# Cross attention: exponentials head by head with a bias, in place of a subtraction on GpSimd

## The reference, cut to what matters

```python
scores = jnp.einsum('bhqd,bhkd->bhqk', Q, K) / np.sqrt(D_K)      # layer 0, D_K = 16
scores = jnp.where(m == 0, NEG, scores)                          # NEG = -1e9
scores = jnp.einsum('bhtd,bhsd->bhts', qh, kh) * scale + mask    # layer 1
attn = jax.nn.softmax(scores, axis=-1)                           # over the 77 context tokens
x = jnp.einsum('bhqk,bhkd->bhqd', attn, V)
```

## Time and profile before

| | us |
|---|---|
| median of 3 runs | 1243.11 (1241.47 to 1243.6) |
| the profiled execution, its own time | 1242.15 |
| span of the trace, first to last instruction | 1240.4 |
| PE busy | 1064.9 (86%) |
| DVE busy | 959.5 (77%) |
| ACT busy | 693.5 (56%) |
| POOL busy | 383.5 (31%) |

### The profile page before, as it was taken

The page is one execution under the profiler, slowest core; times in us unless marked ns, Lnnn a source line. Parts: engine busy times, 40 slices in busy tenths (PEclk is TensorE's granted clock), DMA queues, the critical chain, the costliest instruction groups (busy, mean ns, idle before and its releaser), DMA issues. The chain is left out here.

```text
span 1240.4 us, 30089 instructions
## 1 busy us (share of the span) xinstructions
PE 1064.9 (86%) x10763; PEld 855.5 (69%) x10763; DVE 959.5 (77%) x2126; ACT 693.5 (56%) x1461; POOL 383.5 (31%) x535
## 2 busy tenths in 40 slices
PE   5899989989998799986279999489999859998696
PEld 3578878778787577765267777377788637776585
DVE  7588878877887588997838884569998648898597
ACT  3354544444545255555637776368778626555584
POOL 5123222221230256552220000423421225655232
PEclk9899999999999899997569999699999969999899
DMA  7000000200000230004336531300000000000011
GB/s 263 10 10 2 10 13 2 84 3 2 3 2 2 87 121 12 22 9 174 136 110 246 178 110 49 112 18 19 29 14 21 1 14 24 12 22 10 18 56 47
DMA packets 33493, 64.29 MB, mean 52 GB/s; under 512 B 7524, under 2 KB 23268, under 8 KB 30308
## 3 DMA queue, kind: packets, MB, share of 16 engines
q1 hardware_dynamic: 31844, 58.57, 13.5%
q0 software_dynamic: 1536, 4.20, 1.0%
HBM read 43.03 MB, written 12.39 MB: 45 GB/s over the span
## 5 line engine op out<-in xcount | busy, mean ns | idle before, releaser
L1151 ACT ACTIVATE ca_pth<-ca_turned 77x512 f16<-77x512 f32 x128 | 75.9, 593 | 99.8 <-PE ca_turned L1293 99.8
L395 ACT ACTIVATE wa_probs<-wa_scores,wa_minus_top 128x192 f32<-128x192 f32 x256 | 83.3, 437 | 80.5 <-DVE wa_minus_top L488 80.5
L1094 POOL TENSOR_TENSOR ca_z<-ca_z,ca_top 128x308 f32<-128x308 f32 x128 | 88.2, 701 | 112.4 <-DVE ca_top L1189 112.4
L351 POOL TENSOR_TENSOR wa_q<-wa_by_cos,wa_by_sin 128x256 f32<-128x256 f32 x32 | 23.4, 732 | 265.4 <-DVE wa_by_sin L483 265.4
L1194 DVE SCALAR_TENSOR_TENSOR ca_ptl<-ca_turned,ca_pth 77x512 f16<-77x512 f32 x128 | 87.0, 680 | 20.0 <-ACT ca_pth L1151 20.0
L1293 PE MATMUL ca_turned<-ident,ca_probs 128*77 128x128 f32 x512 | 87.0, 294 | 14.0 <-ACT ca_probs L1143 13.9
L406 ACT ACTIVATE wa_pth<-wa_turned 128x384 f16<-128x384 f32 x128 | 58.4, 506 | 72.2 <-PE wa_turned L715 72.2
L1293 PEld LDWEIGHTS ca_turned<-ident,ca_probs 128*77 128x77 f32 x512 | 57.7, 152 | 44.6 <-ACT ca_probs L1143 24.6
L640 PE MATMUL wa_scores<-wa_xh,wa_wh 128*128 128x256 f16 x256 | 71.1, 278 | 10.4 <-DVE wa_wl L467 8.8
L488 DVE TENSOR_REDUCE wa_minus_top<-wa_scores 128x2 f32<-128x384 f32 x128 | 62.3, 548 | 20.6 <-PE wa_scores L703 18.5
L715 PE MATMUL wa_turned<-ident,wa_probs 128*128 128x128 f32 x512 | 68.3, 275 | 7.8 <-ACT wa_probs L395 3.9
(11 more groups left out here) (388 smaller groups left out, 3643.8 us busy)
## 6 DMA issues: line engine op xcount, KB each, us to landing
ex_stage<-in_ew SPq DMA_DIRECT2D x16, 1024.0 KB, 7.0
slots<-slots_zeros SPq DMA_DIRECT2D x10, 512.0 KB, 6.2
ca_xs<-tokens SPq DMA_DIRECT2D x16, 256.0 KB, 2.4
ex_xe<-slots SPq DMA_DIRECT2D x11, 320.0 KB, 3.3
slots<-ex_y SPq DMA_DIRECT2D x9, 320.0 KB
wa_x_stage<-in_xt SPq DMA_DIRECT2D x8, 256.0 KB, 3.1
tokens<-in_x SPq DMA_DIRECT2D x1, 2048.0 KB, 15.3
ca_w<-in_xw SPq DMA_DIRECT2D x2, 1024.0 KB, 6.9
```

What stands on the lines that cost most here:

```text
L395: ins = act.activation(probs[2 * (u % 2) + t][:, h, t * WINDOW:t * WINDOW + SPAN], s_bank[i][:, t * SPAN:(t + 1) * SPAN], ACT.Exp, bias=mi ...
L1094: pool.tensor_tensor(z[k][:, heads], z[k][:, heads], top[:, k, heads].unsqueeze(2).broadcast_to((P, UH, CTX)), ALU.subtract).then_inc(shif ...
L1151: act.activation(pth[k][0:CTX], t_bank[k][0:CTX], ACT.Copy, scale=PSCALE).then_inc(probs_high, 1)
```

## The change

- POOL's `subtract` is gone, and with it the semaphore `shift`.
- DVE's maximum is written with its sign turned (`negate=True`) into a tile that is now called `minus_top`.
- The exponentials of a unit are four instructions, one for each head (77 values), each with the head's column of `minus_top` as its bias. They wait for the maximum itself (`maxed`). Only the last of the four tells PE (`exped`).
- In layer 0 the factor 1/4 moves from the exponential to the masking, which becomes a `scalar_tensor_tensor` like that of layer 1; the constant for masked scores is then -1e9 in place of -4e9.

```diff
@@ gpsimd
-            def subtract(b, c):
-                pool.wait_ge(maxed, b * PAIRS + c // 2 + 1)
-                k = c // 2 % 2
-                heads = slice(UH * (c % 2), UH * (c % 2 + 1))
-                pool.tensor_tensor(z[k][:, heads], z[k][:, heads], top[:, k, heads].unsqueeze(2).broadcast_to((P, UH, CTX)),
-                                   ALU.subtract).then_inc(shift, 1)
...
-                    if c < UNITS - 2:
-                        subtract(b, c + 2)
-                    elif after:
-                        subtract(b + 1, c + 2 - UNITS)
@@ scalar, power
-                act.wait_ge(shift, b * UNITS + c + 1)
+                act.wait_ge(maxed, b * PAIRS + c // 2 + 1)
                 if not (first(b) and c < 2):
                     act.wait_ge(probs_t, b * UNITS + c - 1)
-                act.activation(probs[k][:], z[c // 2 % 2][:, UH * k:UH * (k + 1)], ACT.Exp, scale=1.0 if additive else CD ** -0.5).then_inc(exped, 1)
+                for h in range(UH):
+                    n = UH * k + h
+                    ins = act.activation(probs[k][:, h], z[c // 2 % 2][:, n], ACT.Exp, bias=minus_top[:, c // 2 % 2, n:n + 1])
+                ins.then_inc(exped, 1)
@@ vector, mask_scores and take_maximum
-                if additive:
-                    ins = dve.scalar_tensor_tensor(out=z[k][:], in0=s, scalar=CD ** -0.5, in1=m, op0=ALU.mult, op1=ALU.add)
-                else:
-                    ins = dve.tensor_tensor(z[k][:], s, m, ALU.min)
-                ins.then_inc(masked, 1)
+                dve.scalar_tensor_tensor(out=z[k][:], in0=s, scalar=CD ** -0.5, in1=m, op0=ALU.mult,
+                                         op1=ALU.add if additive else ALU.min).then_inc(masked, 1)
...
-                dve.tensor_reduce(top[:, k], z[k][:], AX.X, ALU.max).then_inc(maxed, 1)
+                dve.tensor_reduce(minus_top[:, k], z[k][:], AX.X, ALU.max, negate=True).then_inc(maxed, 1)
```

More of the change, by code:

```diff
@@ L801 @@
 PAIRS = UNITS // 2
-MASKED = -4.0e9
+MASKED = -1.0e9
 OPEN = 1.0e38
@@ L1014, in cross_attention @@
         z = [sb(f"z{k}", [P, 2 * UH, CTX]) for k in range(2)]
-        top = sb("top", [P, 2, 2 * UH])
+        minus_top = sb("minus_top", [P, 2, 2 * UH])
         probs = [sb(f"probs{k}", [P, UH, CTX]) for k in range(2)]
@@ L1036, in cross_attention @@
         maxed = sem("maxed")
-        shift = sem("shift")
         exped = sem("exped")
@@ L1117, in batch @@
                         norm.root(pool, b, 0)
-            subtract(0, 0)
-            subtract(0, 1)
             if table:
```

## The result

| | us |
|---|---|
| before, median | 1243.3 |
| after, median of 4 runs | 1289.47 (1285.6 to 1292.78) |
| ratio to before | 1.0376, 95% interval 1.0362 to 1.0391 |
| the profiled execution after: own time, span | 1285.6, 1283.9 |

A forecast was written before the change was run, and what follows sets the result against it. A PE-ACT loop of 1.70 us (turn, ca_pth, exponential, turn) was taken to bound the light units; 1242.15 + 36.8 for longer loops - 2 given back = 1277, plus 0.96 to the median: 1278 us, range 1262 to 1291.

The forecast's parts named there:

- What bounds the kernel: PE and ACT wait for each other in one loop (turn, ca_pth, exponential, next turn) of 1.70 us.
- the light units: Units 0, 2 and 6 of a batch, at the bare loop of 1.70 us, predicted to become 2.35.
- The price of the four exponentials: On ACT, four end 1.10 us after the first starts, against 0.45 for one: +0.65 us in the loop.
- The distances: Turn to turn on PE, each the larger of 2.35 and PE's need; a batch grows from 17.15 to 19.45 us.
- The heavy ones: Distances of 2.46 to 2.54 us, where PE has extra work between turns; predicted to stay as they were.
- that rival: Heavy units get shorter: VectorE's late ca_ptl sets distances of 2.46 to 2.54, which shrink to 2.35; 1267 us, 10%.
- What is given back: Where a loop pass begins, DVE gains time and four late distances shorten by 0.5 us each: -2 us.
- the four late distances: Four batches' distances of 3.02 to 3.06 us where a loop pass begins, 2.52 elsewhere; predicted to lose 0.5 each.
- The clock: Rival: PE idles more and TensorE falls to 1.2 GHz, a batch at least 22.6 us; 1329 us, 5%.
- The range: Whole kernel: 1262 to 1291 us, leaving out the clock, the cheap steps and the not slower case.
- Edits at nothing: Masking with a factor, turned sign on VectorE, and POOL's other work starting earlier were all predicted to cost nothing.
- nobody waits for either: POOL's other work and SP's transfers of the next tokens start earlier, with no engine waiting for them: no effect.

The follow-up runs named there:

- split_only: Changed kernel with the subtraction back on GpSimd and four exponentials per unit of 77 values without a bias column; 1256.66 us, ratio 1.0122 to the kernel before.
- after_second_first: Changed kernel where ACT takes the exponentials of a pair's second unit ahead of ca_pth of the first; 1241.35 us, ratio 0.9987 to the kernel before.
- weigh_twice: Changed kernel with PE doing the twelve small products of weigh twice in units 0, 2 and 6; 1279.91 us, ratio 1.0313 to the kernel before.
- mask_form: Changed kernel with one exponential per unit and the subtraction back on GpSimd, only VectorE's edits left; 1242.97 us, ratio 1.0007 to the kernel before.
- one_exp_apply_late: one_exp with one layer-norm step on VectorE moved from unit 1 to unit 2; 1238.06 us, ratio 0.9964 to the kernel before.
- one_exp: Changed kernel with one exponential per unit (0.02 times the scores), no bias column and no subtraction of the maximum; 1243.01 us, ratio 1.0008 to the kernel before.
- no_bias: Changed kernel with four exponentials of 0.02 times the scores, no bias column and no subtraction; 1252.62 us, ratio 1.0079 to the kernel before.

## Why the prediction was right, and what it missed

- *What bounds the kernel.* Right, and the mechanism with it. The loop of turn, `ca_pth`, exponential, turn sets the light units. split_only and after_second_first show it from both sides: it costs when it grows and pays when it is opened, with ACT's work unchanged.
- *The price of the four exponentials.* Right: 1.10 us predicted, 1.09 to 1.10 measured. The row from SBUF with a bias column was the nearer one, and the Trainium skill's rule ("ScalarE: Activation LUTs", section "What ACT_TABLE_LOAD costs") agrees: 344 ns by it, 347 in the trace, and the 93 ns of the operand are 92 here.
- *The distances.* Seven of eight within 0.06 us, the first within 0.07; a batch is 19.34 to 19.43 against 19.45. The heavy ones shortened by no more than 0.07 us, with 2.2 us more of slack on VectorE, so that rival falls.
- *What is given back.* 3.3 us where I had 2: in the middle batches the four late distances of 3.02 to 3.06 became 2.46, and so did two of 2.73 and the usual 2.53. In weigh_twice, whose profiled execution keeps the full clock in all middle batches, the sum of turns is 310.5 us against 277.1 before, +33.4. Of that 0.8 is its own extra products (four distances of 2.62), so the loops cost 32.6, where I had 34.8. (The kernel before has a stretch of 3.4 us at half clock in each last batch itself, with a distance of 3.85 for 2.47 in one, so the loops may be 1 or 2 us more.)
- *The clock.* This term was put at nothing in the sum, and it is what the 1278 lacks. I priced the clock as all or nothing and gave it 5%, since a stretch with PE busy for 5.90 of 8 us had kept the full clock, and I expected a clock of 1.00. One such row did not bound it. In the profiled execution the clock fell six times between units 7 and 0, 23.1 - 14.8 = 8.3 us. In each last batch it fell for 6.8 us, where weigh_twice has no such stretch, 19.3 - 17.3 = 2.0 twice. That is 12 us in all, and 32.6 + 12 is the 44.7 between the turns. The median of the runs stands 3.9 us above this execution. Their mean clocks fit with more of the same (0.924 and 0.922 at 1285.6 and 1287.1 us, 0.913 at 1291.8 and 1292.8), so of the 46 us between the medians some 14 would be the clock's; that is an estimate, since only one execution has a trace.
- *The range.* That the median fell inside, by 1.5 us, is luck: the range left the clock out, and what came of the clock happened to fit into the room left for dearer exponentials.
- *Edits at nothing.* Right by mask_form for VectorE. For GpSimd's part it was right in the steady batches and in its ground there: the batches of one_exp_apply_late are those of the kernel before. It missed two things. The first batches gain 1.2 to 1.4 us each when one exponential stays one. And "nobody waits for either" of POOL's earlier work left out VectorE, whose layer-norm step ran into the maskings: 5 us between one_exp and one_exp_apply_late. In the changed kernel this step takes up to 1.03 us as well, but the light units are 2.34 there and hide it.

## What to carry to other kernels

When two engines wait for each other in turn, add up one round of that loop from the timeline before asking how busy either is: ACT was busy for 59% of the batch, and each 0.1 us added to it cost the full 0.1 in the light units. Splitting an instruction to save another engine's work has its price: here 0.27 us in the loop for three more pieces, and 0.09 for the column operand of each of the four. Look first for an order in which the piece is off the loop, as here the second unit of a pair, whose input is ready early. And count TensorE's new waits as a risk to its clock.

## What the runs showed of the hardware

*The clock within a busy stage.* Before the drop at 1095.10, PE had been busy for 14.13 of 17.06 us, with waits of up to 1.17 us before its turns; the granted clock then was 0.55 (1.2 GHz for nearly all of it) for 3.8 us, though PE's records fill that stretch. The batches from 1058.62 and from 1159.74 had the same waits and kept 2.4 GHz, so what picks the batch is not shown. With PE busy for 0.9 us more in each batch, by small products (17.32 against 16.42), the profiled execution kept the full 2.4 GHz in all middle batches. The other four executions are known by their times and mean clocks alone, and three of them had a lower mean clock.

*VectorE and GpSimd.* A layer-norm step on VectorE (two column operands, source and result in SBUF, f32) takes 0.40 us, and up to 1.28 in one_exp and 1.44 in no_bias beside GpSimd's tensor-tensor operations. In one_exp each of the long ones ends 0.15 us behind the GpSimd operation. A second operation did the same: `ca_vl`, whose two sources lie in SBUF, takes 0.42 us and up to 1.43 beside a masking, in the kernel before too. The delay goes both ways, as the subtraction of 1.39 us showed. The maximum did not do this: it took 794 to 797 ns in every kernel, also where a GpSimd tensor-tensor operation ran beside it (14 of 62 times in the changed kernel). The Trainium skill ("SBUF — State Buffer", section "Who interferes with whom") describes a pair of ports that the two engines share under a lock, taken for a whole instruction by GpSimd or by a VectorE operation in a two-port mode, and lists tensor_scalar among those and tensor_reduce not. The trace agrees for these two operations. What the runs add: in the kernel before, the subtraction on GpSimd held the masking back until the step had begun, so that the step took 0.40 to 0.45 us, and freeing GpSimd made VectorE slower.
